# Powers and fills moved off GpSimd, and the end of routing re-timed, in a two-layer graph network on one core

## The reference

```python
# layer 0
agg = segment_sum(xn[src], dst)                     # first edge stage
h   = (agg + xn) @ W1 + b1                          # 1024 hidden columns
h   = relu((h - mean(h, 0)) * rsqrt(var(h, 0) + 1e-5) * gamma + beta)
x1  = relu(h @ W2 + b2) + mix                       # mix: linear attention on the nodes
f   = layernorm(x1)
w, e = two best of softmax(relu(f @ rw1) @ rw2)     # 6 experts, routed by row
x2  = x1 + sum_k w_k * expert[e_k](f)               # three 256x256 layers each
# layer 1
xm  = layernorm(x2)
msg = linear maps of xm[src] by edge_attr_4, times an MLP of edge_attr_10 (silu)
x3  = x2 + segment_sum(msg, dst) + attention(xm)    # second edge stage
f3  = layernorm(x3)
out = x3 + layernorm(f3 + two experts of width 512, chosen once for all rows)
```

## Time and profile before

| what | value |
|---|---|
| runs shown | 3272.31, 3272.68, 3282.79 us; median 3272.68 |
| the profiled execution's own time | 3268.49 us |
| its span (first to last instruction) | 3266.9 us |
| busy share of the span | PE 82%, PEld 68%, DVE 51%, ACT 42%, POOL 57% |
| mean granted clock of PE | 0.929 |
| POOL's gathers, first edge stage | 63.5 to 1065.2 us |
| routing | 1098.2 to 1377.5 us |
| jobs, then combine | to 1694.4, then to 1814.2 us |
| POOL's gathers, second edge stage | 1815.0 to 2833.7 us |
| last stage (not changed) | from 2860.8 us |

### The profile page before, as it was taken

The page is one execution under the profiler, slowest core; times in us unless marked ns, Lnnn a source line. Parts: engine busy times, 40 slices in busy tenths (PEclk is TensorE's granted clock), DMA queues, the critical chain, the costliest instruction groups (busy, mean ns, idle before and its releaser), DMA issues. The chain is left out here.

```text
span 3266.9 us, 53785 instructions
## 1 busy us (share of the span) xinstructions
PE 2665.3 (82%) x14861; PEld 2229.0 (68%) x14861; DVE 1678.7 (51%) x5238; ACT 1378.0 (42%) x3900; POOL 1875.1 (57%) x2025
## 2 busy tenths in 40 slices
PE   1888888887888799499972599989888877769998
PEld 1766777777777688388861376666667666758786
DVE  5222236765666466533337365656566666633333
ACT  4222223422212455133335697879645554422221
POOL 5777777777777156433431677777777777500000
PEclk9899999998999899699985799999989999989999
DMA  7644456656666377433338444444446655432221
GB/s 220 174 138 140 135 159 213 183 183 199 195 204 199 110 224 225 107 92 93 96 100 247 146 126 115 125 118 123 121 142 188 172 157 157 141 86 72 66 72 53
DMA packets 303539, 475.05 MB, mean 145 GB/s; under 512 B 100201, under 2 KB 233756, under 8 KB 301914
## 3 DMA queue, kind: packets, MB, share of 16 engines
q0 software_dynamic: 93056, 232.28, 24.6%
q1 hardware_dynamic: 204204, 225.97, 23.7%
q10 hardware_dynamic: 6002, 13.60, 1.2%
HBM read 359.65 MB, written 111.92 MB: 144 GB/s over the span
## 5 line engine op out<-in xcount | busy, mean ns | idle before, releaser
L2337 POOL DMA_INDIRECT g_got<-xm_d,idx x782 | 765.4, 979 | 235.8 <-issue 221.8
L849 POOL DMA_INDIRECT g_got<-xn_d,idx x782 | 757.5, 969 | 238.4 <-issue 228.5
L1143 PE MATMUL ps<-g_hot,g_got 128*128 128x120 f32 (+4 forms) x3128 | 441.6, 290 | 140.8 <-DMA g_got<-xn_d,idx 138.4
L1143 PEld LDWEIGHTS ps<-g_hot,g_got 128*128 128x128 f32 x3128 | 416.1, 203 | 201.3 <-DMA g_got<-xn_d,idx 167.6
L1983 PEld LDWEIGHTS ps<-g_hotw,g_got 128*128 128x128 f32 x3128 | 409.0, 199 | 167.9 <-DMA g_got<-xm_d,idx 83.8
L1983 PE MATMUL ps<-g_hotw,g_got 128*128 128x128 f32 (+11 forms) x3128 | 433.3, 289 | 97.6 <-DMA g_got<-xm_d,idx 63.6
L2390 ACT ACTIVATE g_hotw<-g_hot,g_wr 128x16 f32<-128x16 f32 (+8 forms) x1308 | 302.7, 308 | 167.9 <-DVE g_hot L586 167.1
L1331 POOL TENSOR_TENSOR p_ln_rs<-p_ln_pre,neg_half 125x2 f32<-125x2 f32 x50 | 35.1, 701 | 475.9 <-DVE p_ln_pre L1326 475.9
L2462 DVE TENSOR_TENSOR g_ring<-g_ring,ps 128x84 f32 (+10 forms) x391 | 133.4, 341 | 310.6 <-PE ps L1983 156.7
L1909 POOL DMA_INDIRECT z_d<-p_yj,p_to x108 | 121.5, 1125 | 205.1 <-DVE p_to L1932 183.3
L2778 ACT ACTIVATE p_hid<-ps,p_b 128x250 f32<-128x250 f32 x200 | 82.8, 465 | 279.7 <-PE ps L2740 279.7
(11 more groups left out here) (348 smaller groups left out, 4793.2 us busy)
## 6 DMA issues: line engine op xcount, KB each, us to landing
h_d<-gin_hid SPq DMA_DIRECT2D x23, 1000.0 KB, 5.1
gin_hid<-h_d SPq DMA_DIRECT2D x23, 1000.0 KB
p_xr<-jobs_d SPq DMA_DIRECT2D x54, 258.0 KB, 2.8
g_got<-xn_d,idx POOLq DMA_INDIRECT x782
g_got<-xm_d,idx POOLq DMA_INDIRECT x782
g_half<-xmT_d SPq DMA_DIRECT2D x100, 125.0 KB
p_wj<-z_d SPq DMA_DIRECT2D x50, 224.0 KB
q_d<-g_qo SPq DMA_DIRECT2D x25, 250.0 KB
```

The source lines that it names most:

```text
L849: landed.start(e.indirect_dma_start(got[:, k % (2 * GB), :], None, xn_d[0:N, :], bass.IndirectOffsetOnAxis(ap=idx[:, k:k + 1], axis=0)), k ...
L1143: mm = e.matmul(to, got[:, 2 * (g % GB) + j, c * P:(c + 1) * P], hot[:, g % HR, j, 0:w].unsqueeze(1).broadcast_to([P, r, w]), start=(j == ...
L2337: landed.start(e.indirect_dma_start(got[:, 2 * (g % GB) + j, :], None, xm_d[0:N, :], bass.IndirectOffsetOnAxis(ap=idx[:, 2 * g + j:2 * g + ...
```

## The change

Six parts.

1. First edge stage: `blank_rows`, `blocks` and the two fills ahead of the gathers move from POOL's stream to DVE's, at the same steps. The aggregation of statistics moves into DVE's timeline, one step behind the statistics of each of the four parts of the last block. The power on POOL becomes a square root on ACT and a reciprocal on DVE.
2. Routing: nine pairs and seven single batches. For the last five batches (blocks 20 to 24) the steps stand closer (`near`), and two scatters may share a step. The roots of this stage stay on POOL.
3. Routing: a pad of 256 rows is written by one transfer of whole rows from one tile. All pads now carry the same token numbers, so `address` adds `j * JOB` where a row's rank is 0, and `z_d` grows to 54 jobs of spare rows. The wait for the scatters' landings moves from POOL to SP.
4. Combine: the root is a square root on ACT (`deviation_of`) and a reciprocal on DVE in `shift_of`; ACT's `normed` and `copy` lag by one more step.
5. Second edge stage: the fill of `w1b` and `mask` move to DVE; `roots` becomes ACT's `deviations` at `PAIRS` + 9 and a reciprocal in DVE's `f3_of`; `F3` is 2 steps earlier.
6. The roots of routing and of the last stage are as they were.

```diff
-BATCHES = [*((b, b + 2) for b in range(0, NB - 3, 2)), *((b, b + 1) for b in range(NB - 3, NB))]
+BATCHES = [*((b, b + 2) for b in range(0, NB - 7, 2)), *((b, b + 1) for b in range(NB - 7, NB))]
...
# first edge stage, POOL
-                    timeline(LAST_STEP, (TILES, [(gather, 0)]), ([14], [(blank_rows, 0)]), ([30], [(blocks, 0)]))
-                    e.wait_ge(s_var, 1)
-                    e.tensor_tensor(tmp[:, 1, :], tmp[:, 0, :], neg_half[:, 0:HC], ALU.pow).then_inc(s_inv, 1)
+                    timeline(LAST_STEP, (TILES, [(gather, 0)]))
# ACT
+                    e.wait_ge(s_var, 1)
+                    e.activation(tmp[:, 1, :], tmp[:, 0, :], ACT.Sqrt).then_inc(s_inv, 1)
# DVE
+                    def aggregate(q):
+                        def stage(_):
+                            stat.wait(e, NB - 1, str(q))
+                            for c in (2 * q, 2 * q + 1):
+                                e.bn_aggr(hmv[:, c, :], hst[:, c, :, :].rearrange("p b k -> p (b k)")).then_inc(s_v, 1)
+                        return stage
...
-                             ([4], [(scale_weights, 0)]), ([60], [(message_maps, 0)]),
+                             ([4], [(scale_weights, 0)]), ([60], [(message_maps, 0)]), ([14], [(blank_rows, 0)]), ([30], [(blocks, 0)]),
+                             *((UPQ[q][-1:], [(aggregate(q), 5)]) for q in range(4)),
...
+                    step(e.reciprocal(tmp[:, 0, :], tmp[:, 1, :]))
...
# routing
+            LATE = len(BATCHES) - 5
+            def marks(fn, lag, near):
+                return ([m + (lag if b < LATE else near) for b, m in enumerate(MARKS)], [(fn, 0)])
...
-                    due = max(MARKS[b] + 19, due + 1)
-                    SEND[due] = q
+                    due = max(MARKS[b] + 19, due + 1) if b < LATE else max(MARKS[b] + 17, due + 1 - q % 2)
+                    SEND.append(due)
...
-                e.dma_start(rows[:, :, 0:D], blank[:, :, :]).then_inc(s_pad, 16)
-                e.dma_start(rows[:, :, D:RW], pad[:, b, :, :]).then_inc(s_pad, 16)
+                e.dma_start(jobs_d[ds(at, JOB), :].rearrange("(t p) f -> p t f", t=2), pad[:, :, :]).then_inc(s_pad, 16)
...
-                    timeline(LAST_STEP, (MARKS, [(at_batch(exp_gap), 17), (at_batch(exp_logits), 13)]),
+                    timeline(LAST_STEP, marks(at_batch(exp_gap), 17, 15), marks(at_batch(exp_logits), 13, 12),
-                    timeline(LAST_STEP, (MARKS, [(at_batch(places), 18)]),
+                    timeline(LAST_STEP, marks(at_batch(places), 18, 16),
-                             (MARKS, [(at_batch(place_rows), 19), (at_batch(choose_second), 16),
-                                      (at_batch(choose_first), 14), (at_batch(shift), 12)]))
+                             marks(at_batch(place_rows), 19, 17), marks(at_batch(choose_second), 16, 15),
+                             marks(at_batch(choose_first), 14, 13), marks(at_batch(shift), 12, 12))
...
# combine
-                    pipeline(e, NB, [(copy, 1), (normed, 0)], loop=False)
+                    def deviation_of(i, u, h):
+                        ln.stats.wait(e, i, "pre")
+                        devs.done(e.activation(dev[:, i, :], ln.pre[:, i, :], ACT.Sqrt), "dev")
+                    pipeline(e, NB, [(copy, 2), (normed, 1), (deviation_of, 0)], loop=False)
...
# second edge stage
-            F3 = [P9[b | 1] + 14 + 3 * (b % 2) for b in range(NT)]
+            F3 = [P9[b | 1] + 12 + 3 * (b % 2) for b in range(NT)]
...
-                    timeline(LAST_STEP, (GROUPS, [(gather, 0)]), ([FIRST + 8], [(mask, 0)]), (PAIRS, [(roots, 15)]))
+                    timeline(LAST_STEP, (GROUPS, [(gather, 0)]))
...
+                    def deviations(i):
+                        ln.stats.wait(e, 2 * i + 1, "pre")
+                        ln.norm.wait(e, 2 * i + 1 - XR, "f")
+                        at = slice(2 * i % XR, 2 * i % XR + 2)
+                        spread_of.done(e.activation(ln.rs[:, at, 0], ln.pre[:, at, 0], ACT.Sqrt), "dev")
...
-                             (KV, [(square, 5), (roots, 8)]), (F3, [(copy, 2)]))
+                             (KV, [(square, 5), (roots, 8)]), (PAIRS, [(deviations, 9)]), (F3, [(copy, 2)]))
...
# f3_of, DVE
+                        if i % 2 == 0:
+                            at = slice(i % XR, i % XR + 2)
+                            spread_of.wait(e, i // 2, "dev")
+                            ln.root.done(e.reciprocal(ln.rs[:, at, 0], ln.rs[:, at, 0]), "root")
```

More of the change, by code:

```diff
@@ L1486, in _ @@
                     pad_tails(e, range(0, NE0, 2))
-                    e.wait_ge(s_pad, 32 * NPADS)
+                    e.wait_ge(s_pad, 16 * NPADS)
+                    for r in range(RING):
+                        sent.wait(e, r, (NB - 1 - r) // RING)
                 @block.scalar
@@ L1610, in scatter @@
                             rows1[:, ring(i) + t, :], None), i % RING)
-                    timeline(LAST_STEP, (POS, [(lambda i: ln.roots(e, i, i % 2), 6)]), (list(SEND), [(scatter, 0)]))
-                    for r in range(RING):
-                        sent.wait(e, r, (NB - 1 - r) // RING)
+                    timeline(LAST_STEP, (POS, [(lambda i: ln.roots(e, i, i % 2), 6)]), (SEND[0::2], [(lambda q: scatter(2 * q), 0)]),
+                             (SEND[1::2], [(lambda q: scatter(2 * q + 1), 0)]))
                 @block.vector
@@ L1757, in gps_kernel @@
             goes = ph.sb("goes", [P, YB, 2])
+            past = ph.sb("past", [P, YB, 2])
             to = ph.sb("to", [P, YB, 2], I32)
@@ L1768, in gps_kernel @@
             weights = ph.steps("weights", "w")
-            ids = ph.steps("ids", "goes", "to")
+            ids = ph.steps("ids", "goes", "past", "both", "to")
             turn = ph.steps("turn", "x")
@@ L1912, in _ @@
                     pipeline(e, NJ, [(send, 0)], loop=False)
-                    pipeline(e, NB, [(lambda i, u, h: ln.roots(e, i, i), 0)], loop=False)
                 @block.vector
@@ L1956, in shift_of @@
                     def shift_of(i, u, h):
+                        devs.wait(e, i, "dev")
+                        ln.root.done(e.reciprocal(ln.rs[:, i, :], dev[:, i, :]), "root")
                         ln.root.wait(e, i, "root")
@@ L2235, in gps_kernel @@
             ln = RowNorm(ph, "ln", ("f",), tiles=1, bufs=XR)
+            spread_of = ph.steps("spread", "dev")
             turn = ph.steps("turn", "turn")
```

89 lines of the change are left out of this document (42 added, 47 removed).

## The result

| | before | changed |
|---|---|---|
| median of the runs beside the prediction, us | 3272.68 | 3249.93 (3240.65 to 3255.02) |
| ratio, 95% interval | | 0.9909 [0.9884, 0.9933] |
| profiled execution: own time, span, us | 3268.5, 3266.9 | 3250.6, 3248.8 |
| a second time, beside the experiments, us | 3271.9 | 3241.0, ratio 0.9909 [0.9896, 0.9922] |

The change makes the kernel 0.9% faster: 23 and 31 us in the medians, 18 in the two profiled spans, where the sum of the prediction was 35. To see where they came from, both traces are cut at the same events (first and last gather, last rows of PE, last scatter, and so on) and the stages subtracted. The columns "changed" and "again" of the table are two executions of the same changed kernel; their last stage differs by 12 us, so a single pair of profiles tells less of it than of the others.

The account below looks back on a forecast made before the run. POOL's queue was taken to bound the edge stages, PE most of the others. Terms -6.8 - 3.1 - 5 + 0.6 - 20.7 = -35.0 us took the median from 3272.7 to 3238, range 3224 to 3253.

Parts of the forecast that it names:

- Fills, -6.8: First edge stage: moving fills from POOL to DVE removes holes between gathers and 0.5 ahead of the first; -6.8 us.
- rival C: Fills on DVE hold the gathers as long as they did on POOL; +6.3 us back, 3244; chance 0.05.
- End of the stage, -3.1: End of first edge stage: aggregates between statistics -1.8, root on ACT instead of power on POOL -1.3; -3.1 us.
- Routing, -5: Routing: last places 1 us later, but a shorter scatter queue ends near 1361 against 1366.3; -5 us.
- rival B: Routing's tail doesn't shorten, as single batches and PE's places make the last block late; price 5 to 8, 3244; chance 0.10.
- So +1.6 and not its whole length: Routing: PE's places of block 22, waiting for second choices ahead of the last turn, delay the chain by only 1.6 us.
- Combine, +0.6: Experts and combine: loop unchanged, root hidden in ACT's wait, one table load of 1.28 net of faster roots; +0.6 us.
- Last edge stage, -20.7: Last edge stage: POOL loses a fill 0.5, mask 1.0 and 22 roots 13.9; sums' end -5, f3 lag -0.3.
- so up to 6.6 comes back at the end: Last edge stage: without DVE's coupling to POOL's roots, the sums' 10.5 us lag could shrink to 3.9; -5 taken.
- rival A: DVE becomes the bound of the last edge stage's second half, gaining 11 us instead of 21; 3248; chance 0.15.
- D: Last edge stage: ACT's 37 table loads reach PE and add 47 us, so the kernel is slower, 3285; chance 0.04.
- E: Edge stages: another limit, such as landing, takes the freed pitch; only the ends count, -8 us, 3265; chance 0.03.

Follow-up runs that it names:

- f14_noload_pow: Changed kernel with last edge stage's f3 at lag 14 and Copy for its square root, first edge stage's power back on POOL; 3249.7 us, 0.9926.
- turn_steps: Changed kernel with routing's batches, lags and one scatter a step of before, and PE's turn of f3 one step later; 3229.0 us, 0.9868.
- pool_roots2: Changed kernel with last-stage roots back on POOL, f3 at lag 14, and routing's old lags and one scatter a step, single batches kept; 3248.4 us, 0.9932.
- e5_turn: Changed kernel with PE's turn of f3 in the last edge stage one step later, its copy and store too; slow chip, 3673.0 us, 0.9978.
- f14_steps: Changed kernel with last-stage f3 at lag 14 and routing's batches, lags and one scatter a step of before; 3237.4 us, 0.989.
- e1_steps: Changed kernel with routing's batches, lags and one scatter a step of before, new pads and SP's wait kept; slow chip, 3683.1 us, 1.001.
- dve_less: Changed kernel with DVE work left out of the last edge stage (radial products and sums over 4 of 64 columns from the fourth chunk); 3228.3 us, 0.9864.
- pe_less: Changed kernel with PE work left out of the last edge stage's products (half the mix, the ring's first slice); 3235.2 us, 0.989.
- e4_no_loads: Changed kernel with Copy for the square root in the last edge stage's deviations, so no table loads for it; slow chip, 3682.8 us, 1.0008.

## Why the prediction was right, and where it was not

The time was in the range and the sign right; the forecast of 3238 was 12 below the first median and 3 below the second. The sum is another matter, and its coming out so near is in part luck: 35 us were composed of terms of which two failed, by 8 to 11 and by 7 to 13 us, and four gains were not in it (5 us of shorter gathers in the first edge stage, 2.9 at the hand-over behind it, 3.5 behind the last scatter, 1.8 ahead of the last edge stage's first gather).

*Fills, -6.8.* Right for what lies between gathers: the holes are gone, no gather beside a DVE fill is late, so rival C falls. The 0.5 ahead of the first gather can't be seen: it starts at 63.98 for 63.50, and between 62.95 and 64.09 in all profiles. Nine profiles of this stage show 988.0 to 991.3 us, 12 under the one of before; the shorter gathers that make the other half of it are measured, their cause isn't (of before there is one profile).

*End of the stage, -3.1.* From the last block's first statistic to the end of gin_bias it was 14.15 and is 10.70: -3.45, of it -2.25 for the aggregates (forecast -1.8) and -1.2 for the root (-1.3). Not seen ahead: -2.9 in the hand-over, which f14_noload_pow gave back alone.

*Routing, -5: the step that failed.* It came out at +6.2, and at +3.0 in the second profile; rival B had the sign of the mistake but neither its size nor its place, which is not the tail. "So +1.6 and not its whole length" priced one stop of PE. The trace shows stops of 1.93, 1.71 and 1.44 us inside the last rows, as each late block's choices come due on DVE a few steps ahead of PE, and the granted clock at 0.83 between them: the last five blocks of rows took 54.4 us for 46.4, 5.1 of the 8 in stops. All nine profiles with the short lags have 51.3 to 54.5 us there, all five without them 44.5 to 47.8; with the old lags (turn_steps, pool_roots2) PE doesn't stop for as long as 1.4 us. The clock is the smaller part: in e5_turn it was 1.00 over these blocks, and they took 51.3. The other 3.8 us of the 11.8 lie in the first twenty blocks, and not in the change: kernels with the steps of before have 184.7 to 188.8 us there as well (f14_steps, turn_steps, e1_steps) for 183.3 in the one profile of before. "The queue is short when the last block comes" was wrong too: the root of the last block, with its wait of 3.99, stands in POOL's program ahead of the scatters of the last five blocks, so they still run as one queue. The places came 2.6 nearer to the last rows and the last scatter only 1.9; with single batches and the old lags it is 35.2 us behind the rows as well (pool_roots2), so the short lags bought nothing there. The 3.5 us between the last scatter and the next stage were not in the sum; all thirteen other profiles have 6.9 to 8.2 us there for 11.2, and all of their kernels have the new pads and SP's wait, which weren't undone by themselves, so their cause stays open.

*Combine, +0.6.* It was -0.5; the root lies in ACT's wait, and the loop stays at 4.15 a block. The 2.6 in front of the first gather are 0.8 of the fill and 1.8 that no run separated; POOL's last root ended 11.7 us ahead of the next stage there, so it isn't the case of f14_noload_pow.

*Last edge stage, -20.7: the other step that failed.* Its first half held: POOL's stretch shrank by 9 to 18 us over five profiles, 14.4 in the mean of 1004.3, for 14.9. In the changed kernel none of the 782 gathers stands more than 0.45 us behind the one before, where 23 did before, with 15.4 us in all beyond the 0.30 of an issue; what scatters is the gathers' own mean, 976 to 987 ns. The second half, "so up to 6.6 comes back at the end", named the wrong cause of the lag. The wait for the first root is there, but it only comes first: at group 240 the sums lag by 17 us before and 15 in pool_roots2, and by 6 to 9 in the kernels with roots on ACT; at group 300 it is 21 and 20 for 20 to 28 (12 in dve_less). Worked out from the gathers' and sums' ends, PE's sums fall behind between groups 200 and 300 in every version: at 2.81 us a group before, for POOL's 2.63, and at 2.78 and 2.70 in the changed kernel's two profiles, for POOL's 2.57 and 2.55. That is DVE: 2.62 in dve_less, 2.74 in pe_less. So the lag grew from 10.5 to between 12 and 20, as rival A said, with its mechanism and nearly its price (11 us for 21; the stage gave 2 and 15 in two profiles, 7 in the mean of five). How long DVE's work holds PE depends on the order: with the turn of f3 a step later the next sums don't stand behind it, and the stage is 1024, 5 and 17 us under the changed kernel's two profiles and 12 under the mean (lag 9.0), as e5_turn was 12 under e4_no_loads on the slow chip. The busy time of DVE, 291 of 428 us, did not show it; 71 us in front of its additions, where the program loads a register, and 45 of waiting for PE fill most of the rest.

*Rivals D and E.* D is refuted: without the loads the stage is 3 us shorter, and 6 on the slow chip, where D's price was 47. In the changed kernel ACT waits 77 us for one-hots and 68 for PE between 2380 and 2808 us, so it had them to give. The Trainium skill, "ScalarE: Activation LUTs", section "What ACT_TABLE_LOAD costs", gives 1283 ns for a load and about 2.66 us with its drain, an estimate of 98 us for the 37. The trace agrees on the load, 1283 ns for each, and not on the drain: the next activation starts 0.01 to 0.02 us behind it. E falls on the chips of the forecast. On the slow one another limit did take the freed pitch, as E says, but it was not the landing that it names.

## What to carry to other kernels

Taking work off the queue that paces a stage pays until the next engine is as late: ask for the rate of that next engine in the densest stretch, group by group, not for its busy share over the stage. Steps moved closer together at the end of a stage put in-order engines into each other's waits; a stop of PE costs its length and, in eight of nine profiles here, a lower clock behind it, so first see what the queue at the very end is really waiting for. And keep POOL's computing out of the last microsecond or two of a stage: here it cost 2.9 us beside its own time.

## What the runs showed of the hardware that was not expected

- Where a compute instruction of POOL (a power, 1.66 and 1.68 us) ended 0.7 us ahead of the stage's last instruction, which is DVE's, the next stage's first instructions on POOL, ACT and DVE came 4.4 to 4.5 us behind that last one, twice; where POOL had done nothing but gathers and had been idle for over 20 us, 1.5 to 1.6 us, in twelve profiles. So 2.9 us for a POOL instruction just ahead of the hand-over.
- On one chip the same gathers, issued 1.26 us apart while there was room, were paced to a mean of 1.52 to 1.57 us by late sums: the gathers' stretches of the edge stages took 1195 and 1228 us (e1_steps) for 990 and 1004, while experts and combine took the same time as elsewhere. The gathers' packets were moved in time, and DVE, ACT and POOL were as busy as elsewhere; PE, at a granted clock of 0.86 for 0.93, was busy 963 us of the last edge stage for 884 and idle for 289 for 143, and no run shows why. The 14 us of roots that POOL gave up were worth nothing there.
- Two executions of one program differ by 12 us in the last edge stage alone, while the expert stage repeats within 1 us.
